# Pseudo-inverse through E = I - A on sixteen value columns, and the last attention's inputs image by image

## The reference, cut to what matters

```
v = (1 / max(sum(k, rows))) * k.T
for _ in range(6):
    kv = k @ v
    v = 0.25 * v @ (13 I - kv @ (15 I - kv @ (7 I - kv)))
out = softmax1 @ (v @ (softmax3 @ V)) + conv(V)
```

## Time and profile before

| | us |
|---|---|
| median of 3 runs | 1401.24 |
| lowest, highest | 1397.11, 1401.38 |
| profiled execution, its own time | 1398.71 |
| its span, first to last instruction | 1396.9 |

### The profile page before, as it was taken

How to read it: one execution, slowest core, us unless ns; L and a number is a source line. 1 busy time by engine, 2 the same in 40 slices (tenths; PEclk the granted TensorE clock), 3 DMA queues, 4 the chain that set the end, 5 groups by cost and what they waited for, 6 DMA issues and landing times. The chain is left out here.

```text
span 1396.9 us, 22443 instructions
## 1 busy us (share of the span) xinstructions
PE 1077.9 (77%) x7858; PEld 821.9 (59%) x7859; DVE 612.5 (44%) x1443; ACT 435.3 (31%) x878; POOL 303.7 (22%) x497
## 2 busy tenths in 40 slices
PE   6895999969987779989972079997474899752991
PEld 5694888855566568879962036665353455441770
DVE  4743655531145646566555024443354577330112
ACT  3651455533222224433210011110233366410330
POOL 4543201111011110000141700000574212114004
PEclk9956999999999889989975579999677799855996
DMA  7446634100230010000047211111133332142644
GB/s 93 116 115 153 154 70 101 35 2 24 68 77 3 0 45 2 1 2 1 2 133 202 79 40 46 56 47 41 42 86 94 110 98 71 33 98 68 172 139 101
DMA packets 121920, 98.45 MB, mean 70 GB/s; under 512 B 32499, under 2 KB 113453, under 8 KB 121197
## 3 DMA queue, kind: packets, MB, share of 16 engines
q1 hardware_dynamic: 114967, 87.30, 24.6%
q0 software_dynamic: 4608, 9.44, 2.4%
q10 hardware_dynamic: 2261, 0.59, 0.2%
HBM read 69.86 MB, written 35.20 MB: 75 GB/s over the span
## 5 line engine op out<-in xcount | busy, mean ns | idle before, releaser
L991 DVE TENSOR_REDUCE l3a_nmax<-l3a_psS 128x2 f32<-128x512 f32 x96 | 62.8, 686 | 40.2 <-PE l3a_psS L845 40.2
L1347 DVE TENSOR_REDUCE l0a_nmax<-l0a_psS 98x2 f32<-98x392 f32 x96 | 54.2, 567 | 54.4 <-PE l0a_psS L1162 50.4
L947 ACT ACTIVATE l3a_PT<-l3a_psST 128x512 f32<-128x512 f32 x96 | 54.8, 596 | 30.8 <-PE l3a_psST L875 30.4
L2615 PEld LDWEIGHTS l2e_psY<-W2T,l2e_HT 128*128 128x128 f32 x320 | 51.5, 190 | 19.2 <-issue 19.1
L2635 ACT ACTIVATE l2e_H<-l2e_psH 128x512 f32<-128x512 f32 x40 | 21.7, 595 | 131.6 <-PE l2e_psH L2597 131.6
L2615 PE MATMUL l2e_psY<-W2T,l2e_HT 128*128 x320 | 57.3, 332 | 4.0 <-issue 2.3
L1297 ACT ACTIVATE l0a_PT<-l0a_psST 98x392 f32<-98x392 f32 x96 | 47.2, 497 | 42.2 <-PE l0a_psST L1204 41.9
L2583 PE MATMUL l2e_psX<-ident,l2e_X 128*128 128x128 f32 x40 | 8.1, 284 | 59.1 <-DMA l2e_X<-xs 59.1
L194 PE MATMUL l3p_psT<-ident,l3p_xn 128*96 128x128 f32 x32 | 8.0, 425 | 49.4 <-DVE l3p_xn L184 49.4
L2080 PE MATMUL l2i_ps<-l2i_D,l2i_A 96*96 96x96 f32 x512 | 44.5, 248 | 0.0
L2080 PEld LDWEIGHTS l2i_ps<-l2i_D,l2i_A 96*96 96x96 f32 x512 | 44.0, 165 | 0.0
(11 more groups left out here) (528 smaller groups left out, 2951.0 us busy)
## 6 DMA issues: line engine op xcount, KB each, us to landing
l3a_QS<-qd SPq DMA_DIRECT2D x72, 64.0 KB, 2.4
l3a_KS<-kd SPq DMA_DIRECT2D x72, 64.0 KB, 2.4
expert_W<-in_L_ffn_w SPq DMA_DIRECT2D x8, 576.0 KB, 4.1
rd<-l0q_r_p SPq DMA_DIRECT2D x24, 168.0 KB
xs<-const_zeros SPq DMA_DIRECT2D x4, 960.0 KB, 10.3
l2e_X<-xs SPq DMA_DIRECT2D x20, 192.0 KB, 2.5
ys<-l2e_Y SPq DMA_DIRECT2D x20, 192.0 KB, 2.0
l0a_QS<-qd SPq DMA_DIRECT2D x54, 64.0 KB
```

Of the source, the lines that this page charges most:

```text
L947: nc.scalar.activation(PT[n % 3][:, s, :], psST[item % 2][:, :], ACT.Exp).then_inc(exp_done, 1)
L991: nc.vector.tensor_reduce(nmax[k % 2][:, TI * u:TI * (u + 1), s], psS[item % 2][:, :].rearrange("p (t k) -> p t k", t=TI), AX.X, ALU.max, ...
L1347: mx = nc.vector.tensor_reduce(nmax[k % 2][0:WQ, 2 * j:2 * (j + 1), s], psS[item % 2][0:WQ, 0:2 * W0].rearrange("p (t k) -> p t k", t=2), ...
L2615: mm = nc.tensor.matmul(psY[:, t * C:(t + 1) * C], HT[b][t][:, mb, :], W2T[:, bass.ds(e * NM + mb, 1), :].rearrange("p a c -> p (a c)"), s ...
```

## The change

In the inverse, A stays symmetric, and so does E = I - A. One iteration becomes E' = E^2 (3 E + E^2) / 4, and for the values X' = (E^2 (4 X + E X)) / 4 + X + E X. X starts as the 16 value columns of each head (K3 compressed, K3C) over the column maximum and is kept beside E in one tile U of 112 columns. A turn is two products of 112 columns: U2 = E U = [E^2 | E X], then E^2 D with D = [3 E + E^2 | 4 X + E X]. The last turn's second product has 16 columns; the final product is K2^T X, 16 columns, spread over the blocks by a mask. V, VT, A and `eyes` go.

In the inputs, each turn is one image; each of the 32 gathers has its own buffer, the code is written out in place of loops, the third pieces go from GpSimd to DVE (`Pieces.third`) and V's copy from DVE to ScalarE. TensorE turns image i+1 between Q, K and V of image i; DVE normalises i+1 before the rests of i and adds i+2 before the thirds of i.

```diff
 l2_inverse, tensor
-            product(LO, K2T, Vm, a_mm, (v_done, 0))
-            for it in range(ITERATIONS):
-                at = NBK * it
-                product(HI, A, D7, b_mm, (d7_done, at))
-                product(LO, A, D15, c_mm, (d15_done, at), (vt_done, at))
-                if it < LAST - 1:
-                    product(HI, A, D13, a_mm, (d13_done, at))
-                    product(LO, D13, VT, vt_mm, (d13_done, at))
...
-            product(LO, VT, K3, mb_mm, (vt_done, NBK * ITERATIONS))
+            for b in range(NBK):
+                pe.wait_ge(v0_done, b + 1)
+                product(b, 0, K2T, lambda g: V0[:, g, :], CH).then_inc(a0_mm, 1)
+            for k in range(ITERATIONS):
+                for b in range(NBK):
...
+                        pe.wait_ge(e_done, NBK * (k - 1) + b + 1)
+                        pe.wait_ge(x_done, NBK * (k - 1) + b + 1)
+                    product(b, 0, U, lambda g: U[:, g, :], WIDE).then_inc(sq_mm, 1)
+                for b in range(NBK):
+                    pe.wait_ge(u2_done, NBK * k + b + 1)
+                    pe.wait_ge(d_done, NBK * k + b + 1)
+                    cols = needed(k)
+                    product(b, 4, U2, lambda g: D[:, g, cols], cols.stop - cols.start).then_inc(q_mm, 1)
+            for b in range(NBK):
+                pe.wait_ge(x_done, NBK * LAST + b + 1)
+                product(b, 0, K2, lambda g: U[:, g, X], LM).then_inc(mb_mm, 1)
 scalar
+            for k in range(ITERATIONS):
+                for b in range(NBK):
+                    act.wait_ge(sq_mm, NBK * k + b + 1)
+                    nc.scalar.activation(U2[:, gs(b), :], bank(b, WIDE), ACT.Copy).then_inc(u2_done, 1)
+                for b in range(NBK if k < LAST else 0):
+                    act.wait_ge(q_mm, NBK * k + b + 1)
+                    act.wait_ge(x_done, NBK * k + b + 1)
+                    nc.scalar.activation(U[:, gs(b), EB], bank(4 + b, WIDE)[:, :, EB], ACT.Copy, scale=0.25).then_inc(e_done, 1)
 vector
+            nc.vector.tensor_reduce(K3C[:], K3[:].rearrange("p g (h m) -> p g m h", h=HB), AX.X, ALU.add).then_inc(k3c_done, 1)
...
+            for k in range(ITERATIONS):
...
+                    if k < LAST:
+                        nc.vector.scalar_tensor_tensor(D[:, gs(b), EB], U[:, gs(b), EB], 3.0, U2[:, gs(b), EB], ALU.mult, ALU.add)
+                    nc.vector.scalar_tensor_tensor(D[:, gs(b), X], U[:, gs(b), X], 4.0, U2[:, gs(b), X], ALU.mult, ALU.add).then_inc(d_done, 1)
+                nc.vector.tensor_tensor(S[:], U[:, :, X], U2[:, :, X], ALU.add).then_inc(s_done, 1)
...
+                    nc.vector.scalar_tensor_tensor(U[:, gs(b), X], bank(4 + b, n)[:, :, n - LM:], 0.25, S[:, gs(b), :], ALU.mult, ALU.add).then_inc(x_done, 1)
+            for b in range(NBK):
+                dve.wait_ge(mb_mm, b + 1)
+                nc.vector.tensor_tensor(of_heads(MB[:, gs(b), :]), free(ps[b][0:CH, 0:1], [LM, GB], [0, HB], [1, LM]), masks(GB), ALU.mult).then_inc(mb_done, 1)
 combined_inputs in place of attention_inputs and Combined
+        Y = [[st.sb(f"Y{t}{k}", [P, C]) for k in range(2)] for t in range(NT)]
 gpsimd
+            stats.init(pool)
+            gather(0)
+            for i in range(B):
+                if i + 1 < B:
+                    gather(i + 1)
+                stats.gpsimd(nc, pool, i, i % 2)
 scalar
+            nm.scalar(nc, act, 0, 0)
+            for i in range(B):
+                u = i % 2
+                evacuate(i, u, psQ, QF, qp, q_mm, q_free, 1.0)
+                qp.scalar(nc, act, QF[u][:, :, :], i, u, (q_free, i + 1))
+                evacuate(i, u, psK, KF, kp, k_mm, k_free, HD ** -0.5)
+                if i + 1 < B:
+                    nm.scalar(nc, act, i + 1, 1 - u)
+                kp.scalar(nc, act, KF[u][:, :, :], i, u, (k_free, i + 1))
+                qp.second(nc, act, i, u)
+                act.wait_ge(nm.xT_free, i + 3)
+                nc.scalar.activation(VA[:, TI * i:TI * (i + 1), :, 0:HD], psV[u][:, 0:2 * C].rearrange("p (t h d) -> p t h d", t=2, h=NH), ACT.Copy).then_inc(v_free, 1)
+                kp.second(nc, act, i, u)
 vector
+            combine(0)
+            combine(1)
+            norm(0)
+            for i in range(B):
+                u = i % 2
+                if i + 1 < B:
+                    norm(i + 1)
+                qp.vector(nc, dve, QF[u][:, :, :], i, u)
+                kp.vector(nc, dve, KF[u][:, :, :], i, u)
+                if i + 2 < B:
+                    combine(i + 2)
+                qp.third(nc, dve, i, u)
+                kp.third(nc, dve, i, u)
```

More of the change, by code:

```diff
@@ L289, in image_of @@
     return bass.AP(tensor=base.tensor, offset=base.offset, ap=[list(d) for d in dims])
[L292 to L414, removed]
@@ L2066, in l2_inverse, with product @@
         NBK = NG // GB
-        bank = lambda b: ps[b][0:CH, 0:GB * CH].rearrange("p (g c) -> p g c", g=GB)
-        gs = lambda b: slice(b * GB, (b + 1) * GB)
         ITERATIONS = 6
         LAST = ITERATIONS - 1
+        gs = lambda b: slice(b * GB, (b + 1) * GB)
+        bank = lambda b, n: ps[b][0:CH, 0:GB * n].rearrange("p (g c) -> p g c", g=GB)
+        EB, X = slice(0, CH), slice(CH, WIDE)
+        needed = lambda k: slice(0, WIDE) if k < LAST else X
         @block.tensor
         def _(pe):
-            def product(b0, lhs, rhs, done, *gates):
-                for b in range(NBK):
-                    for s, at in gates:
-                        pe.wait_ge(s, at + b + 1)
-                    for g in range(b * GB, (b + 1) * GB):
-                        mm = nc.tensor.matmul(ps[b0 + b][0:CH, (g % GB) * CH:(g % GB + 1) * CH], lhs[:, g, :], rhs[:, g, :], start=True, stop=True)
-                    mm.then_inc(done, 1)
+            def product(b, b0, lhs, rhs, n):
+                for g in range(b * GB, (b + 1) * GB):
+                    mm = nc.tensor.matmul(ps[b0 + b][0:CH, (g % GB) * n:(g % GB + 1) * n], lhs[:, g, 0:CH], rhs(g), start=True, stop=True)
+                return mm
             pe.wait_ge(sm, 5)
@@ L2159, in _ @@
+            nc.vector.tensor_reduce(K3C[:], K3[:].rearrange("p g (h m) -> p g m h", h=HB), AX.X, ALU.add).then_inc(k3c_done, 1)
+            dve.wait_ge(k3c_done, 1)
+            nc.vector.tensor_tensor(U[:, :, X], K3C[:], free(inv[:, 0:1], [1, NG], [0, LM]), ALU.mult).then_inc(x0_done, 1)
             for b in range(NBK):
-                nc.vector.tensor_tensor(VT[:, gs(b), :], K2[:, gs(b), :], scale(b), ALU.mult).then_inc(vt_done, 1)
-            def minus(dst, src, k, gate, at, done):
-                for b in range(NBK):
-                    dve.wait_ge(gate, at + b + 1)
-                    nc.vector.scalar_tensor_tensor(dst[:, gs(b), :], src(b), -1.0, free(eyes[:, k, 0:1], [0, GB], [1, CH]), ALU.mult, ALU.add).then_inc(done, 1)
@@ new lines, in combined_inputs, with _, gather, turn @@
+def combined_inputs(nc, G, eps):
+    with Stage(nc, "l3p") as st:
+        W, VA = G["full"]["W"], G["VA"]
+        Y = [[st.sb(f"Y{t}{k}", [P, C]) for k in range(2)] for t in range(NT)]
+        KF, QF = ([st.sb(f"{n}{u}", [CH, 2, T]) for u in range(2)] for n in ("KF", "QF"))
+        stats, nm = LnStats(st, G, eps), Normed(st, G)
+        qp, kp = Pieces(st, G, "q", CH, (2, T)), Pieces(st, G, "k", CH, (2, T))
+        psQ, psK = st.ps("psQ"), st.ps("psK")
+        psV = [st.ps(f"psV{u}") for u in range(2)]
+        y_in = [st.sem(f"y_in{t}") for t in range(NT)]
+        added, pads_done, q_mm, q_free, k_mm, k_free, v_free = st.sems("added pads_done q_mm q_free k_mm k_free v_free")
+        block = st.block()
+        @block.sync
+        def _(sp):
+            for i in range(B):
+                for pieces, dst in ((qp, G["qd"]), (kp, G["kd"])):
+                    pieces.sync(sp, rows(dst, i // 2 * 3 * C * 2 * T + i % 2 * T, [2 * T, CH], [2 * C * T, 3], [2 * CH * T, 2], [1, T]), i, i % 2)
+            qp.finish(sp)
+            kp.finish(sp)
+        @block.gpsimd
+        def _(pool):
+            def gather(i):
+                for t in range(TI * i, TI * (i + 1)):
+                    for k in range(2):
+                        pool.indirect_dma_start(out=Y[t][k][:, :], out_offset=None, in_=G["ys"],
+                                                in_offset=bass.IndirectOffsetOnAxis(ap=G["slots"][k][:, t:t + 1], axis=0)).then_inc(y_in[t], 16)
+            stats.init(pool)
[4 more added lines that the diff above has]
+                stats.gpsimd(nc, pool, i, i % 2)
+        @block.tensor
+        def _(pe):
+            nm.init_credit(pe)
+            def turn(i):
+                nm.tensor(nc, pe, i, i % 2)
+            def project(i):
+                u = i % 2
+                pe.wait_ge(nm.xT_done, i + 3)
+                for ps, m0, freed, done in ((psQ, 0, q_free, q_mm), (psK, 2, k_free, k_mm)):
+                    if i:
+                        pe.wait_ge(freed, i)
+                    for a in range(2):
+                        for k in range(2):
```

(53 more changed lines are left out.)

121 lines of the change are left out of this document (34 added, 87 removed).

## The result

| | before | after |
|---|---|---|
| median, us | 1400.39 (4 runs, 1397.11 to 1401.38) | 1349.93 (4 runs, 1346.57 to 1353.59) |
| profiled execution, its span | 1398.71, 1396.9 | 1350.03, 1348.1 |
| inverse: its first operation to the next stage's first matmul | 80.6 | 54.3 |
| the stage behind it, to the router's first normalisation | 23.5 | 25.8 |
| the inputs' stage: GpSimd's first operation to the last store | 105.3 | 81.3 |

The ratio is 0.9648, 95% interval 0.9623 to 0.9672. The prediction said 1347, range 1335 to 1366. Of the 48.8 us between the spans the inverse gave 26.3, the inputs 24.0, and the stage behind the inverse took 2.3 back; the rest, 0.8, lies in stages that are the same.

What follows compares the result with a forecast made beforehand. The prediction took TensorE to bound the inverse and waits between engines the inputs' stage. Gains of 29.4 and 24.4 us, 53.8 off 1398.71, gave 1344.9, plus 2.5 to the median: 1347 us, range 1335 to 1366.

Steps and rivals of the forecast that it cites:

- TensorE bounds the inverse, a turn is two wide products: Inverse: TensorE busy throughout, each turn two products of 112 columns at 3.12 us, five turns 31.2 us.
- The copy chain is hidden by 0.35 us: Inverse turns: copies and DVE steps end at t + 5.9 us, before TensorE's second product at t + 6.24.
- Rival C: Inverse: the copy chain takes TensorE's place, 1.2 us late a turn, five turns cost 6 more, 1353 us; chance 0.11.
- The opening: Inverse's start: nothing moves, with K3C at 1.75 us; if K3C takes 3.5 us, 1.2 us are lost.
- The end: Inverse's tail: MB done 8.2 us after the last squaring, at 662.8, with 16-column records 68 ns apart.
- the sign that I had set: Inverse: forecast right if its stretch is 39 to 41 us from the first squaring.
- The inputs: Inputs' stage: a loop over engines of 8.4 us an image, last store at 1055.1 for 1079.50, gain 24.4 us.
- B: Inputs' stage: TensorE stays at half clock, 10.7 us an image, gain 3 there, 1369 us in all; chance 0.12.
- D: Inputs' stage: DVE's two-input operations and GpSimd's gathers hold each other up, 19.6 us an image, 1406; chance 0.02 slower, 0.01 same.
- E: Inputs' stage: GpSimd's 6.6 to 7 us an image is the bound, 5 x 1.6 less, 1339 us; chance 0.12.
- The sum: Whole kernel: 29.4 + 24.4 = 53.8 us off 1398.71 gives 1344.9; median 2.5 above the profiled execution, so 1347.

Runs made afterwards that it cites:

- s_three: New kernel with the inverse's sum S over 256 columns computed three times a turn, two into an unread tile; 1348.95 us, 6.62 us a turn.
- wide_both: New kernel with the inverse's last second product and final product both moving 112 columns instead of 16; 1346.34 us, ratio 0.9621 to the old kernel.
- eight_buffers: New kernel with the 32 gathers sharing eight buffers as before; 1351.92 us, ratio 0.9633 to the old kernel, inputs' stage 82.2 us.
- thirds_gpsimd: New kernel with the third pieces back on GpSimd, two images late in its order; 1362.09 us, ratio 0.9735 to the old kernel.
- adds_first: New kernel with DVE's adds and statistics of image i+2 ahead of the rests of image i; 1338.62 us, ratio 0.9566 to the old kernel.

## Why the prediction was right, and where it was off

- **TensorE bounds the inverse, a turn is two wide products.** Right: 36.40 of 36.40 us busy. A wide product was priced at 3.12 and costs 3.07 ((3.23 - 0.26) / 31 = 96 ns a record); five turns 0.5 us better.
- **The copy chain is hidden by 0.35 us.** Right: 0.4 by s_three, and in the new kernel E of bank 0 is copied 0.4 us before the next squaring's weights load (640.45 + 0.42 = 640.87, for 641.28). Rival C is out.
- **The opening.** K3C took 2.73, between the 1.75 taken and the 3.5 of the bound; the first squaring comes 0.4 us later from the stage's start than B did.
- **The end: the term that was mis-sized.** Forecast 8.2 us from the last squaring to MB, measured 664.94 - 653.54 = 11.4 (the squaring's weights start there). Two terms make the 3.2. A 16-column record costs 83 ns, not 68, which is 1 us for the two products: four records of another stage were too few to read an interval from, and I had named 85 as the far end. And the last product ran at half clock, 4.98 us for 2.81, which is 2.2. By the sign that I had set, 39 to 41 us from the first squaring to MB, the inverse missed: 664.94 - 622.89 = 42.1.
- **What comes behind.** No step looked at the clock in which the inverse leaves the next stage: 2.3 us. With the end this makes the inverse's part 24.0 net where 29.4 was forecast. wide_both shows the cause, and gives 3.7 back.
- **The inputs.** 24.0 us for 24.4. The loop was named in its order and lasts 8.03, forecast 8.4; the cold beginning cost 1.5 more than forecast and the tail 0.6 more (1031.04 - 1021.3 = 9.7), so errors of both signs cancel in the 24.0. Its sum needed no gain from the buffers, but the text listed them first among the reasons; eight_buffers shows that they count for little.
- **Rivals B and D.** The stage's clock is 0.80 of full, between the levels; Q's 8 records take 1.89 in five of the eight images and 2.48 to 3.73 in the others, so B's half clock is there at times, but the loop hardly feels it (RSTD 8.0 to 8.2 us apart behind the cold beginning). DVE's adds stay at 408 ns, but GpSimd's statistics are stretched beside DVE's third pieces (L160 0.46 for 0.22, L162 1.02 for 0.72). The rule quoted from the Trainium skill (GPSIMD Engine Reference, section 8, Key points) holds, at some 0.5 us an image in the new kernel. As quoted, for two SBUF inputs, it does not cover the normalisation of thirds_gpsimd, which has one tensor input and took 1002 ns for 389.
- **E.** GpSimd's own pace was not reached; adds_first gets near it, and its gain of 7.8 is about what E had asked for (8).
- **The sum, and luck.** By the stages the forecast was 5.8 us too good (53.8 for 48.0), nearly all of it in the inverse's end and behind it. That the median still came within 3 us of 1347 is in part luck: 0.8 us came from other stages, and the sum added 2.5 us from a profiled execution to a median, where the new kernel's median lies 0.1 below its own profiled execution. A slip in the working, (1.89 - 0.25) / 7 = 0.22, should read 0.23; it enters only the far end of the price of a wide record.

## What to carry to other kernels

Narrowing a product's moving side below its weights' columns buys nothing (83 ns for 16 columns, 85 for 96) and here cost the clock for that product and the stage behind; price the stage behind a tail as well. Where no engine is busy throughout, write down the loop through the engines in program order: its sum gave the period within 5%, and taking its longest member out of it was worth more than the buffers (7.8 us for 0.9). A piece of elementwise work on GpSimd cost twice here, once itself and once on the DVE operation that happened to stand beside it.

## What was not expected of the hardware

TensorE's clock fell from 2.4 to 1.2 GHz while TensorE was busy for 2.70 of 2.70 us by the records (windows 656.6 to 662.0), with records of 16 columns and no idle time; with 112 columns in the same places it stayed up. Busy records did not hold the clock here. When it falls differs from one profile to the next: over the six with both products narrow the last product took 3.26 us (eight_buffers) to 5.21 (adds_first), and the inverse and the stage behind it together 79.7 to 80.2, but for s_three with its longer turns. Why narrow columns bring the clock down no run here shows.
